# Cross-attention over 16 sequences: from the second sequence on, scores are issued ahead of the value matmuls and of t

## What is computed

```python
mu, var = mean and variance of input over channels and positions
xn = (input - mu) * rsqrt(var + 1e-5) * gamma + beta
q = Wq @ xn + bq ; k, v = split(Wkv @ context + bkv)
att = softmax((q * c**-0.25) @ (k * c**-0.25).T)     # per head, 256 x 256
out = Wo @ (att @ v) + bo
return input + out
```

## Time and profile before

| what | us |
|---|---|
| median of 3 runs | 228.94 |
| lowest, highest run | 227.13, 229.73 |
| profiled execution, first to last instruction (span) | 228.2 |
| PE busy | 208.6 (91%) |
| DVE busy | 199.3 (87%) |
| ACT busy | 181.1 (79%) |
| POOL busy | 160.3 (70%) |

### The profile page before, as it was taken

The page is one execution under the profiler, slowest core; times in us unless marked ns, Lnnn a source line. Parts: engine busy times, 40 slices in busy tenths (PEclk is TensorE's granted clock), DMA queues, the critical chain, the costliest instruction groups (busy, mean ns, idle before and its releaser), DMA issues.

```text
span 228.2 us, 7194 instructions
## 1 busy us (share of the span) xinstructions
PE 208.6 (91%) x2511; PEld 179.9 (79%) x2511; DVE 199.3 (87%) x589; ACT 181.1 (79%) x371; POOL 160.3 (70%) x157
## 2 busy tenths in 40 slices
PE   6968878799999999999999998999999999999872
PEld 6857757588888798889888887888888888887761
DVE  3589987879898999899999999999999998989765
ACT  2374586787889988898889888989897979888880
POOL 5135185777987877789788887789686869776460
PEclk9975897999999999999999999999999999999998
DMA  5964137480767566566665665656657656442000
GB/s 134 261 272 93 27 82 174 107 184 14 164 141 160 131 153 142 132 141 151 140 153 122 160 151 121 151 127 154 142 127 166 149 133 143 93 94 62 13 3 23
DMA packets 31090, 29.04 MB, mean 127 GB/s; under 512 B 4240, under 2 KB 29840, under 8 KB 31056
## 3 DMA queue, kind: packets, MB, share of 16 engines
q1 hardware_dynamic: 30224, 28.07, 52.4%
q10 hardware_dynamic: 832, 0.53, 1.0%
HBM read 3.80 MB, written 1.05 MB: 21 GB/s over the span
## 4 chain that ended last, share of the span: by engine, by line
PE 41%; POOL 20%; issue 13%; ACT 11%; DVE 11%; ACTq 2%; POOLq 0%; DVEq 0%
POOL p_lo L773 19%; PE ps_sc L522 6%; PE ps_max L546 6%; PE ps_sc L523 5%; PE ps_z L479 4%; ACT p_full L678 4%; DVE neg_max L894 4%; ACT p_hi L675 3%; PE ps_z L481 3%; PE ps_z L480 3%; PE ps_z L414 3%; PE ps_m L589 2%; PE ps_t L497 2%; PE ps_m L590 2%; DVE z_sum L910 2%
## 5 line engine op out<-in xcount | busy, mean ns | idle before, releaser
L773 POOL TENSOR_TENSOR p_lo<-p_full,p_hi 128x512 f16<-128x512 f32 x122 | 139.9, 1163 | 42.3 <-ACT p_full L678 41.2
L675 ACT ACTIVATE p_hi<-ps_sc 128x512 f16<-128x512 f32 x128 | 77.9, 608 | 18.3 <-PE ps_sc L523 15.9
L894 DVE TENSOR_REDUCE neg_max<-ps_max 128x2 f32<-128x512 f32 x128 | 85.9, 677 | 6.9 <-PE ps_max L546 6.8
L678 ACT ACTIVATE p_full<-ps_sc 128x512 f32<-128x512 f32 x128 | 78.7, 615 | 0.0
L522 PE MATMUL ps_sc<-t_a,c_seq 128*128 128x256 f32 x256 | 71.2, 300 | 3.5 <-issue 2.6
L523 PE MATMUL ps_sc<-t_b,c_seq 65*128 65x256 f32 x256 | 67.3, 284 | 0.0
L479 PEld LDWEIGHTS ps_z<-u_hi,p_hi 128*128 128x128 f16 x512 | 46.4, 97 | 12.8 <-issue 8.2
L479 PE MATMUL ps_z<-u_hi,p_hi 128*128 128x65 f16 x512 | 53.0, 195 | 2.2 <-DVE p_lo L930 1.9
L522 PEld LDWEIGHTS ps_sc<-t_a,c_seq 128*128 128x128 f32 x256 | 49.2, 192 | 5.9 <-issue 4.6
L480 PE MATMUL ps_z<-u_lo,p_hi 128*128 128x64 f16 x512 | 52.8, 193 | 0.0
L481 PE MATMUL ps_z<-u_hi,p_lo 128*128 128x65 f16 x512 | 52.7, 194 | 0.0
(11 more groups left out here) (108 smaller groups left out, 233.9 us busy)
## 6 DMA issues: line engine op xcount, KB each, us to landing
t_a<-t_a SPq DMA_DIRECT2D x90, 128.0 KB, 2.4
t_b<-t_b SPq DMA_DIRECT2D x30, 128.0 KB, 2.5
x_seq<-x_hi SPq DMA_DIRECT2D x15, 128.0 KB, 2.4
c_pad<-c_hi SPq DMA_DIRECT2D x30, 64.0 KB, 2.1
c_seq<-c_hi SPq DMA_DIRECT2D x15, 128.0 KB, 2.4
x_res<-x_tiles SPq DMA_DIRECT2D x4, 256.0 KB, 6.7
out<-x_res SPq DMA_DIRECT2D x16, 64.0 KB, 2.0
x_seq<-x_lo SPq DMA_DIRECT2D x15, 64.0 KB, 2.1
```

Of the source, the lines that this page charges most:

```text
L675: nc.scalar.activation(p_hi[:, buf, :, :].rearrange("p t s -> p (t s)"), scores, ACT.Exp).then_inc(act_phi, 1)
L678: nc.scalar.activation(p_full[:, head % 2, :], scores, ACT.Exp).then_inc(act_p, 1)
L773: nc.gpsimd.tensor_tensor(p_lo[:, buf, :, :].rearrange("p t s -> p (t s)"), p_full[:, head % 2, :], p_hi[:, buf, :, :].rearrange("p t s -> ...
L894: nc.vector.tensor_reduce(to, ps_max[:, unit % 2, :].rearrange("p (t s) -> p t s", t=KT), X, ALU.max, negate=True).then_inc(dve_max, 1)
```

## The change

In both engines the step is cut into named parts. For n below 1 the parts stand as before. From n = 1 on PE issues scores, then value matmuls, then t, and ACT does its exponentials, then the copy of t. The rest of the step (M, Y, U, the transpose; ACT's u and transposed maxima) comes behind as before. DVE, POOL and SP are untouched, and so are all waits.

```diff
@@ PE
-            def step(n, h):
+            def values(n, h):
                 if e := av_at(n, h):
...
+            def queries(n, h):
+
                 for turn, m, k in t_at(n, h):
...
+            def scores(n, h):
 
                 if e := at(n, h, 0):
...
+            def step(n, h):
+
+                if n < 1:
+                    values(n, h)
+                    queries(n, h)
+                    scores(n, h)
+                else:
+                    scores(n, h)
+                    values(n, h)
+                    queries(n, h)
+
                 for m, unit in max_at(n, h):
@@ ACT
-            def step(n, h):
+            def query_copies(n, h):
 
                 for turn, m, k in t_at(n, h):
...
+            def exponentials(n, h):
+
                 if e := at(n, h, 0):
...
+            def step(n, h):
+
+                if n < 1:
+                    query_copies(n, h)
+                    exponentials(n, h)
+                else:
+                    exponentials(n, h)
+                    query_copies(n, h)
 
                 if e := u_at(n, h):
```

More of the change, by code:

```diff
@@ L671, in step @@
                     buf = head % P_BUFS
-                    scores = ps_sc[:, head % 2, :]
+                    bank = ps_sc[:, head % 2, :]
                     act.wait_ge(pe_s2, m * H + head + 1)
                     need(act, pe_av, m * H + head + 1 - P_BUFS)
-                    nc.scalar.activation(p_hi[:, buf, :, :].rearrange("p t s -> p (t s)"), scores, ACT.Exp).then_inc(act_phi, 1)
+                    nc.scalar.activation(p_hi[:, buf, :, :].rearrange("p t s -> p (t s)"), bank, ACT.Exp).then_inc(act_phi, 1)
                     if m > 0 or head >= 2:
                         lo_done(act, m, head - 2)
-                    nc.scalar.activation(p_full[:, head % 2, :], scores, ACT.Exp).then_inc(act_p, 1)
+                    nc.scalar.activation(p_full[:, head % 2, :], bank, ACT.Exp).then_inc(act_p, 1)
+            def step(n, h):
[5 more added lines that the diff above has]
+                    query_copies(n, h)
                 if e := u_at(n, h):
```

## The result

The changed kernel took 236.97 us in the median (235.27 to 238.7, 4 runs) against 229.33 (227.13 to 230.47, 4 runs): a ratio of 1.043, 95% interval 1.033 to 1.054. Forecast were 235.5 us and a range of 230.0 to 241.5. The profiled execution has a span of 236.9 us against 228.2.

What follows compares the result with a forecast made beforehand. A ring through PE (busy 91%) and DVE sets the pace, with a ring through the maxima row's DMA beside it. Span 228.2 + 8.9 for the sequences - 1.7 for the tail = 235.4, so 235.5 us; range 230.0 to 241.5.

Steps and rivals of the forecast that it cites:

- The main term: At h = 0, S0 moves 1.28 us earlier; V0 and T0 (0.73, 0.55 us) no longer hide the maxima row's DMA.
- S0 to M0: PE's stretch at h = 0 after the row lands: 0.48 us before, 1.84 us after the change.
- the formula of 9.94 plus landing: Time per sequence: 0.96 to issue, landing, 0.1 to S0, 1.84 to M0, 7.04 to the next transpose.
- The landing: Time for the DMA of the row of maxima to land after issue; the old mean of 2.56 us was taken over.
- the rival of the short landing: Row lands in about 2.0 us nearly always: 227.6 us, half way 231.5, standing for 227 to 231; chance 0.14.
- T behind V: The copy of t ends later, so M1 waits 0.13 us and restarts with 0.1; charged 0.06, bounds 0 and 0.23.
- The ring through DVE and PE: The loop of PE and DVE work said to set the pace, 11.5 us when the row lands within 1.6 us.
- The 0.12 us that I gave back for DVE: u_hi comes 0.26 us earlier, so DVE is no longer late for M0's maximum: 0.12 us gained per sequence.
- The tail: In the last sequence S2 goes directly behind Y1, the last exponential starting about 1.7 us earlier; bounds 0 and 2.2.
- Faster: Rival: ACT's idle times set the pace, so only 0.12 us per sequence and the tail count: 224.8 us; chance 0.05.
- Long landings: Rival: copies of t, now closer, hold the maxima row, 3.2 us on average, 244 us; chance 0.11.
- The wait for the copy of t: Rival: M1 loses 0.23 us per sequence instead of 0.06, 2.4 us more, 237.8; counted within the forecast's 0.70.

Runs made afterwards that it cites:

- run 1: Changed kernel with h = 0 kept in the old order on PE and ACT; ratio 0.986 to the kernel before, median 229.03 us.
- run 2: Changed kernel with the new order only at h = 0, old order at the other steps; ratio 1.060 to the kernel before, 243.84 us.
- run 8: The changed kernel once more, unaltered, one execution, to look at the clock; 236.01 us, span 234.2.
- run 10: Changed kernel, heads 0 and 1 taking their second scores product from t_a with 65 rows, the maxima row awaited only ahead of S2; ratio 1.006, 229.19 us.
- run 3: Changed kernel with the new order only from the last sequence on, old order before; ratio 0.988 to the kernel before, median 227.42 us.
- run 4: Changed kernel, but at h = 0 PE issues V, S, T; ratio 1.037 to the kernel before, 238.52 us.
- run 5: Changed kernel, scores of heads 0 and 1 leaving out the maxima row (64 rows instead of 65), its DMA awaited only ahead of S2; ratio 1.055.
- run 6: Kernel before, scores of heads 0 and 1 leaving out the maxima row (64 rows instead of 65), its DMA awaited only ahead of S2; ratio 1.056.
- run 11: Kernel before, heads 0 and 1 taking their second scores product from t_a with 65 rows, the maxima row awaited only ahead of S2; ratio 0.996, 226.96 us.
- run 7: Changed order on PE, but ACT keeps the copy of t ahead of the exponentials; ratio 1.103 to the kernel before, 253.62 us.

## Why the prediction was right, step by step

**The main term was right in kind and place.** S0 moved ahead of the work that covered the DMA, V0 and T0 came behind its wait, and the sequence follows the landing one for one; sequence 2, where S0 did not wait, and sequences 3 and 7 do not. The table shows it from both sides: 7.8 to 9.4 us of wait in the new order against at most 2.7 in the old. Runs 1 and 2 put the loss at h = 0, but for 0.1 us in a sequence at h = 2.

**Sizes on the ring.** Issue after the transpose: predicted 0.96, measured 0.91. S0 to M0: 1.84, measured 1.84 to 1.85 in eleven of fourteen sequences. M0 to the transpose: 7.04, measured 7.08 to 7.17 where nothing else came in. In sequences 4, 6, 8 and 10 to 13 the formula of 9.94 plus landing was right within 0.07 us. It leaves out what sequences 1, 3, 5 and 7 have beside it, and had before: a DMA issued later (1.50 and 1.71 us after the transpose in 1 and 5) and a longer way from M0 to the transpose (7.54 us in 3, 7.24 in 7). That sequences without a late DMA repeat 11.64 us to 0.1 was misread: sequences 3 and 7 took 12.11 and 11.81.

**The landing was the unknown, and came out shorter.** I had kept the old mean of 2.56 us; the new one is 2.36, its median 1.9 instead of 2.3. Over the thirteen of sequences 1 to 14 in which S0 waited that is 2.2 us less. The landing thus went a third of the way to the rival of the short landing. With only that, the time would have been near 233.2. That issuing nearer to the copies of t lengthens it is not borne out: in the eight traces in which ACT has the new order at h = 4, so that the DMA is issued early and near to them, the median landing is 1.90 to 2.29 us, in the six others 2.17 to 2.58. Why is open; the means, 2.36 to 2.69 in all fourteen, are ruled by the late rows. Some sequences land late whatever the order: sequence 9 took 2.8 to 3.7 us in all fourteen traces, and sequence 5 at least 2.5. What they collide with was not found. The Trainium skill, "DMA: Bandwidth & Descriptors", section "Anatomy of one DMA — SWDGE (gpsimd) path", gives 2.0 us for so small a transfer, an estimate from its fit, which was made for DMAs that GpSimd issues, not ACT as here. The median of 1.9 agrees with it, the landings of 3.2 to 3.7 do not.

**What was missed: the clock.** Sequence 9 idled 1.73 us ahead of S0 and came back at half clock. The stretches of the changed kernel (columns as in run 8):

```profile
145.40:147.60 2.20, 0.47 (x3) 0.06 (x2) 1.97 (x7) 2.07 (x5) 2.00 (x2) 1.00 0.62 142
147.60:149.00 1.40, 1.40 (x12) 1.31 (x13) 0.11 (x1) 0.20 (x1) 0.26 (x1) 0.52 0.37 91
149.00:151.00 2.00, 2.00 (x26) 2.00 (x24) 0.18 (x1) 0.89 (x2) 1.04 (x1) 0.50 0.31 73
151.00:153.00 2.00, 1.96 (x19) 1.62 (x18) 1.58 (x6) 1.71 (x4) 0.12 (x1) 0.99 0.00 0
```

These are 1.2 GHz in place of 2.4 for 3 us. S0 to M0 took 3.31 us instead of 1.84, so this fall cost 1.5 us. Sequence 1 lost 1.0 the same way. Sequence 5 idled 1.8 us and kept its clock. I had written that the middle stays at full clock; that step failed. In the kernel before no such fall followed one of these waits, the longest of them 1.66 us.

**What was mis-sized: T behind V.** I charged 0.06 us for M1's wait on the copy of t and called the one at h = 4 hidden. In the changed kernel M1 starts 0.97 us after M0, so it lost 0.25, a little more than my upper bound of 0.23, and at h = 4 the transpose came 1.25 after M4 instead of 1.19, since M5 was late as well. The ring through DVE and PE, which I gave 11.5 us, takes 11.85 without the wait (run 10). The 0.12 us that I gave back for DVE did come: M0's maximum started 175.46, 0.43 after M0. But PE had become the later one. The timeline of DVE in the changed kernel:

```profile
174.42 0.69 DVE L950 TENSOR_TENSOR u_lo<-ps_m,u_hi 128x512 f16<-128x512 f32 x1 [0.25 <-ACT u_hi L711]
...
175.46 0.69 DVE L920 TENSOR_REDUCE neg_max<-ps_max 128x2 f32<-128x512 f32 x1 [0.26 <-PE ps_max L561]
```

Half of the wait for u_hi is gone, and DVE waits for M0 instead, as forecast, with nothing won.

**The tail** was predicted at -1.7 us and measured at -1.4 (-1.2 in run 3). ACT's last exponential of the changed kernel starts at 230.42, 11.8 us after the last transpose of the maxima; before it was 13.1, so it came 1.3 earlier and not 1.7:

```profile
230.42 0.59 ACT L695 ACTIVATE p_full<-ps_sc 128x512 f32<-128x512 f32 x1
```

**Which errors cancelled.** The forecast for the span was +7.2 us, measured +8.7. Shorter landings (-2.2), an earlier issue (-0.6) and a slip of mine (-0.5) stood against two falls of the clock (+2.5), +2.1 between M0 and the transpose (the wait for the copy of t, half of it in sequences 1 and 7) and +0.3 in the tail; this comes to the 8.7 within 0.1. The slip: I took S0 to M0 as 0.48 us before in every sequence, but it was 0.55 in those that already waited. So the forecast was right by its mechanism, and close in size partly by luck, because a miss on either side met.

**The rivals.** Faster: would have needed a landing within 1.6 us; the shortest was 1.8. Long landings: in no trace; the highest mean was 2.69 us (run 4), against 3.2. The wait for the copy of t: real, 0.1 us in most sequences of the changed kernel and 0.5 in sequences 3 and 7, and decisive in run 4.

## What to carry to other kernels

Before moving an operation forward, list every semaphore it waits for and read how much spare time each has in the trace: here the scores of one step in eight waited for a DMA with 0.1 to 1.0 us to spare, and the move took away 1.28. A static order can differ by step: the new order did no harm, and in the tail gained 1.2 to 1.4 us, where no late transfer meets it (h = 4 and 6, and the last sequence), and costs 4% when it is applied to all. When an engine's order is turned, the engine that serves it must be checked with it: ACT's order alone made the difference between a ratio of 1.043 and one of 1.103.

## What the runs showed of the hardware

A matmul on 64 rows between two on 128 rows held up its neighbours: starts 0.31 us apart (run 5) instead of 0.12 for the same 256 columns with 65 rows. Two heads of eight in that form made the kernel 5% slower (runs 5 and 6), while with 65 rows it was within 1% of the kernel before (runs 10 and 11). And the clock fell to half behind an idle spell of PE of 1.6 to 1.9 us in some sequences (1 and 9 in the changed kernel, 5 in run 8, 10 in run 7) and stayed full behind spells as long or longer in others, up to 2.46 us.
